# Attention pass of a graph network: who frees the PSUM buffer of the running maximum

## The reference

```python
for i in range(L):                                   # L = 4
    Q = _ln(h @ Wq[i], gq[i], bq[i])
    K = _ln(h @ Wk[i], gk[i], bk[i])
    qi, kj = Q[src], K[dst]
    score = (qi * kj).sum(-1) + 0.1 * (edge_attr * qi[:, :RBF]).sum(-1) + logm[dst]
    smax = jax.ops.segment_max(score, src, num_segments=N)
    es = jnp.exp(jnp.minimum(score - smax[src], 20.0))
    denom = jax.ops.segment_sum(es, src, num_segments=N)
    alpha = es / (denom[src] + 1e-10)
    m = h[dst] @ Wm[i]
    aggi = jax.ops.segment_sum(alpha[:, None] * m, src, num_segments=N)
    ...
```

## Time and profile before

| | us |
|---|---|
| median of 3 runs | 21067.08 |
| profiled execution, its time | 21034.33 |
| profiled execution, its span | 21032.7 |
| DVE busy | 11429.2 (54%) |
| PE busy | 11005.1 (52%) |
| POOL busy | 9367.2 (45%) |
| ACT busy | 4877.2 (23%) |

### The profile page before, as it was taken

How to read it: one execution, slowest core, us unless ns; L and a number is a source line. 1 busy time by engine, 2 the same in 40 slices (tenths; PEclk the granted TensorE clock), 3 DMA queues, 4 the chain that set the end, 5 groups by cost and what they waited for, 6 DMA issues and landing times. The chain is left out here.

```text
span 21032.7 us, 411461 instructions
## 1 busy us (share of the span) xinstructions
PE 11005.1 (52%) x122618; PEld 8580.4 (41%) x122618; DVE 11429.2 (54%) x28337; ACT 4877.2 (23%) x14465; POOL 9367.2 (45%) x10949
## 2 busy tenths in 40 slices
PE   1000056666666558847875884787155555433333
PEld 1000033333333148746865784686133333223233
DVE  4055045555555738865883886588223323256758
ACT  0000022222222034424432442443022222211110
POOL 5677755555555014413431441343344444465370
PEclk9995555555555569968986997898566666655556
DMA  8986544444445354425434442643111111134334
GB/s 60 91 178 145 61 63 63 64 66 65 64 64 66 70 157 121 122 69 174 122 91 146 125 123 65 178 123 95 54 38 37 42 38 40 34 103 131 120 114 130
DMA packets 2671465, 1951.71 MB, mean 93 GB/s; under 512 B 787834, under 2 KB 2449042, under 8 KB 2670285
## 3 DMA queue, kind: packets, MB, share of 16 engines
q1 hardware_dynamic: 1922578, 1150.35, 22.3%
q0 software_dynamic: 309216, 536.66, 14.9%
q10 hardware_dynamic: 439512, 262.80, 6.4%
HBM read 1287.52 MB, written 723.39 MB: 96 GB/s over the span
## 5 line engine op out<-in xcount | busy, mean ns | idle before, releaser
L592 POOL DMA_INDIRECT edges_rows<-raw,edges_perm_now x1824 | 1871.0, 1026 | 1582.8 <-DVEq L1163 626.0
L592 POOL DMA_INDIRECT attend_rows<-key_rows,attend_fetch_now x1824 | 1826.8, 1002 | 1047.8 <-POOL attend_fetch_now L1573 724.6
L592 POOL DMA_INDIRECT keys_rows<-table,keys_staged x1564 | 1683.5, 1076 | 548.2 <-issue 483.6
L1638 PE MATMUL attend_seg<-attend_rows,attend_hot 128*128 128x49 f32 x14592 | 1808.3, 278 | 70.1 <-issue 47.9
L1638 PEld LDWEIGHTS attend_seg<-attend_rows,attend_hot 128*128 128x128 f32 x14592 | 1720.6, 194 | 100.7 <-issue 82.0
L592 POOL DMA_INDIRECT mlp_xin<-table,mlp_staged x1564 | 1520.4, 972 | 499.4 <-issue 463.7
L1693 DVE TENSOR_REDUCE attend_mraw<-attend_top 128x2 f32<-128x1024 f32 x912 | 1114.1, 1222 | 531.0 <-remote 343.1
L2281 DVE COPY mlp_val<-mlp_ps 128x192 f32<-128x192 f32 (+1 forms) x414 | 143.3, 346 | 2295.4 <-DMA hots_lanes<-dst_lanes 1328.6
L598 POOL DMA_INDIRECT messages<-spread_out,spread_place_now x912 | 1202.0, 1318 | 394.3 <-issue 340.2
L1025 PE MATMUL edges_ps<-edges_w,edges_act 49*128 49x48 f32 x3648 | 870.9, 411 | 910.0 <-ACT edges_act L1096 872.3
L1025 PEld LDWEIGHTS edges_ps<-edges_w,edges_act 49*128 49x128 f32 x3648 | 810.6, 324 | 959.4 <-issue 958.5
(11 more groups left out here) (511 smaller groups left out, 26390.2 us busy)
## 6 DMA issues: line engine op xcount, KB each, us to landing
key_rows<-expand_out ACTq DMA_DIRECT2D x304, 624.0 KB
attend_ea<-edge_attrs SPq DMA_DIRECT2D x912, 160.0 KB
tally_rows<-messages SPq DMA_DIRECT2D x152, 864.0 KB, 4.8
expand_oht<-dst_hots SPq DMA_DIRECT2D x304, 384.0 KB, 3.5
attend_oht<-src_hots SPq DMA_DIRECT2D x912, 128.0 KB
attend_lane_hot<-src_hots_by_edge SPq DMA_DIRECT2D x912, 128.0 KB
raw<-keys_rows ACTq DMA_DIRECT2D x46, 1445.0 KB
messages<-keys_zeros SPq DMA_DIRECT2D x171, 384.0 KB
```

The source lines that it names most:

```text
L592: return nc.gpsimd.indirect_dma_start(out=out, out_offset=None, in_=table, in_offset=bass.IndirectOffsetOnAxis(ap=index, axis=0))
L1638: ins = mm(seg2[:, u, 0:SUMS], hot[p % 2][:, u, c, :], rows4[p][:, u, c, 0:SUMS], start=(c == 0), stop=(c == GR - 1))
```

## The change

A new semaphore `s_free` is raised by the maximum (L1693) itself. PE's far matmuls wait for it rather than for `s_most`. The maximum no longer counts in DVE's chain, so L1696 doesn't wait for it; L1698, which reads `mraw`, gets a wait for `s_free` of its own. The number of chained instructions in six steps falls from 8 to 7 each. `s_most`, and PE's wait for it before `back` (L1623), stay.

```diff
-        s_step, s_now, ..., s_dve_turn, s_act_turn = (ph.sem(n) for n in (
+        s_step, s_now, ..., s_dve_turn, s_act_turn, s_free = (ph.sem(n) for n in (
...
                     if live(n, 1):
                         p = (b - 1) % RING
-                        after(pe, s_most, n - 1)
+                        after(pe, s_free, n - 1)
                         pe.sem_inc(s_pe_turn, 1)
                         for u in range(2):
                             mm(top[:, u, :].rearrange("m (c q) -> m c q", c=GR), k.far[:], ..., start=True, stop=False)
...
                     if live(n, 1):
                         dve.wait_ge(s_top, n)
-                        ch.step(v.tensor_reduce(mraw[:], top[:], AX, ALU.max))
+                        v.tensor_reduce(mraw[:], top[:], AX, ALU.max).then_inc(s_free, 1)
                     ch.wait()
                     if live(n, 0):
                         ch.step(v.tensor_reduce(score[b % 3][:]...., prod[:]...., AX, ALU.add))
                     if live(n, 1):
+                        dve.wait_ge(s_free, n)
                         ch.step(v.tensor_scalar(mb[one][:, :, 0], mraw[:], -FAR_OFF, None, ALU.add))
...
-                n0, per = ch.n, 8 * RING
+                n0, per = ch.n, 7 * RING
```

More of the change, by code:

```diff
@@ L1547, in attend @@
         back, seg = ph.ps("back", [P, 512]), ph.ps("seg", [P, 512])
-        s_step, s_now, s_q, s_score, s_top, s_most, s_back, s_arg, s_exp, s_hot, s_seg, s_ev, s_table, s_pe_turn, s_pool_turn, s_share, s_hota, s_dve_turn, s_act_turn = (ph.sem(n) for n in (
-            "s_step", "s_now", "s_q", "s_score", "s_top", "s_most", "s_back", "s_arg", "s_exp", "s_hot", "s_seg", "s_ev", "s_table", "s_pe_turn", "s_pool_turn", "s_share", "s_hota", "s_dve_turn", "s_act_turn"))
+        s_step, s_now, s_q, s_score, s_top, s_most, s_back, s_arg, s_exp, s_hot, s_seg, s_ev, s_table, s_pe_turn, s_pool_turn, s_share, s_hota, s_dve_turn, s_act_turn, s_free = (ph.sem(n) for n in (
+            "s_step", "s_now", "s_q", "s_score", "s_top", "s_most", "s_back", "s_arg", "s_exp", "s_hot", "s_seg", "s_ev", "s_table", "s_pe_turn", "s_pool_turn", "s_share", "s_hota", "s_dve_turn", "s_act_turn", "s_free"))
         s_load, s_rows, s_lane = ([ph.sem(f"{n}{b}") for b in ring] for n in ("s_load", "s_rows", "s_lane"))
```

## The result

| | before, median of 6 | after, median of 6 | ratio (95% interval) |
|---|---|---|---|
| time, us | 21055.97 (21031.45 to 21076.49) | 20953.34 (20919.5 to 21006.24) | 0.9953 (0.9936 to 0.9971) |

The change gains 103 us, or 0.47%; the forecast was 55 us (0.26%). The profiled execution of after is its slowest of the six: 21006.24 us, span 21004.6. It began its first attention pass 37 us later than the execution of before did (first maximum at 7917.5, before at 7880.3), in stages that the change doesn't touch, so the spans don't show the gain. The attention passes do: over the same kind of windows as in the earlier trace rows they sum to 4702 us, against 4786.

The account below looks back on a forecast made before the run. A two-step ring of waits through POOL's second gather was taken to bound the attention passes. DVE's earlier L1696 gave 52 us, steps not held 3, the rest 0: 55 us off 21067, so 21012 us, range 20870 to 21120.

Parts of the forecast that it names:

- The ring through the second gather: Attention passes: a two-step ring of waits, maximum, ex, seg, second gather, maximum, sets the pace: 10.43 us for two steps.
- a gather is a bystander: Drawn from the skill's SBUF rule: POOL's gathers wouldn't delay the maximum, and rival 1's plain reading would hold.
- Far's move: PE's far waits for the maximum, not L1710; top starts 0.33 us earlier in step B, but price on the ring 0.
- Rival 1: Plain chain: top's start sets the maximum; 183 us gain, 20884 us, chance 0.12; whole wait gone, 20540 us, 0.03.
- rival 4: s_most (L1623) or s_score (L1614) holds PE as before; time is that of the forecast, chance 0.58 together with it.
- L1696 earlier by 0.115 us: DVE: with the maximum off the chain, L1696 and all behind it up to L1724 come 0.115 us earlier; bounds 0 to 0.12.
- Rival 2: DVE's L1696 stays or gains only 0.034 us: 0 to 16 us, 21051 to 21067 us; chance 0.13.
- The wait at L1698: DVE's new wait for s_free, covered by about 0.8 us of L1696: priced 0, from 0 to 0.18 us.
- Rival 3: The new wait holds L1698 and all behind it by 0.18 us: 82 us slower, 21149 us; chance 0.10.
- the share of steps that no gather holds: Some 5% of the attention steps gain the whole 0.115 us: 3 us more.
- the ring has DVE's part once in two steps: Attention passes: 0.115 us counts half, 0.058 us per step, times 912 steps: 52 us.
- The forecast's own sign: Profile after: idle time before the maximum grows from 527 us by about 50, as the ring gives back half of DVE's gain.

Follow-up runs that it names:

- the moved gather: Kernel after, with POOL's second gather of a step issued only behind back: 20798.04 us, ratio 0.9795; same edit in kernel before, other chip: 18795.02 us, ratio 1.0073.
- the silent POOL: Kernel after without POOL's gathers in the attention passes, SP fetching other rows: 18500.35 us, ratio 0.9914; on a signal-holding chip 20295.76 us, ratio 0.9632.
- the whole: The kernel after, unchanged, run once more beside its two halves, against the kernel before: 21093.58 us, ratio 0.9934.
- the vector engine's half: Kernel after, but far waits for s_most again; the maximum stays out of DVE's chain: 21116.99 us against 21229.0 before, ratio 0.9945.
- the control: Kernel before's order, with L1696 waiting for s_free as well as the chain and far for s_most: 18720.36 us against 18660.16 before, ratio 1.0029.
- the first group: Runs on one chip of both halves, the kernel after and its second gather moved; the kernel before took 21229 us there.
- the matrix engine's half: Kernel after, but L1696 waits for s_free too; far released early: 21352.45 us, ratio 1.0058 to before; once more on another chip 18707.25 us, ratio 1.0019.
- the third group: Kernel after and kernel after without POOL's gathers, on a chip that holds signals: 20983.74 and 20295.76 us against 21072.88 before.
- the second and the last group: Groups on chips that don't hold signals; the kernel before took 18660 us in each.

## Why the prediction was right, and where its size was off

What bounds the kernel: right, for the chips on which it was measured. The ring through the second gather was read from the order in time alone; the moved gather and the silent POOL show that the gathers are the cause of the wait. The Trainium skill's page SBUF — State Buffer, section "SBUF: two separate sides", says that PE never waits on anyone. It says so of the ports to that memory, and PE's matmuls are indeed no slower on the first chip (those of top 220 ns, on the second 219); what comes late is their signal, of which the section says nothing. What the prediction drew from it, that a gather is a bystander, fits the second chip and not the first, where the measurement decides. That a chip could do one or the other I hadn't thought of.

Far's move, priced at 0: right within what the runs can tell. Its wait went from 536.8 us to 8.2, and the idle time before the maximum didn't fall. The half alone gained nothing, and the whole is 23 us ahead of the vector engine's half, within noise. Rival 1, at 183 us, is out. Of rival 4 a part is true, at no cost in time: PE now waits for the score instead (337.1 us of L1716, in the result's rows).

L1696 earlier by 0.115 us: right. From the starts in the trace it follows the maximum by 1.140 us in the mean rather than 1.256, and its idle time is gone. Rival 2 is out: without the wait the next reduction starts 0.08 us before the first has ended, with a wait 0.03 us after. The Trainium skill's page VectorE: DVE Perf Modes, section "The DRAIN you can't avoid", measured that a semaphore between two copies costs nothing extra. The same section also says that a next instruction that isn't held starts earlier, which the prediction left out; for this pair of reductions the trace agrees with that, and not with the first.

The wait at L1698 (now L1699), priced at 0: right. The row of L1699 has no idle time before it. Rival 3 is out; the control shows what a wait costs in front of L1696, where nothing covers it: 0.068 us a step.

The term that was mis-sized is the share of steps that no gather holds, 5% and 3 us of the sum, for which no row was given, and with it "the ring has DVE's part once in two steps" as the whole of the gain. The sum gave 55 us; 103, 135 and 89 us were measured, the lower ends of their intervals at 61, 102 and 63 us. Had the ring alone counted, the idle time before the maximum would have grown by some 50 us, half of the 105 us that L1696 comes earlier in all; it grew by 15. The forecast's own sign was missed there.

I took the ring apart over all pairs of steps, from the starts in both traces. From a maximum to the start of seg it is 4.465 us before and 4.326 after: 0.139 less, about 0.12 of it on DVE, the rest on ACT. In one of two steps that is 63 us over the passes, near the forecast's 52. From seg's end to the next maximum but one it is 3.988 and 3.931, where I had taken no change: another 26 us. The two make 89 of the 97 us that the passes gained.

That second piece is a mean of two kinds: held (about 4.05 us, 92% of the cases before, 90% after) and not held (under 3.9 us, 6.4% and 9.9%). In the other traces on such chips the share of steps not held is 19.3% and 12.1% (the two later ones of after), 12.0% (the vector engine's half) and 1.9% (the matrix engine's half, in which DVE is slower). So my 5% isn't a constant. That the change raises it is argued only: there is one trace of before on such a chip, and three of the same kernel after lie between 9.9% and 19.3%. On the one chip of the first group the kernel with the slower DVE has 1.9% of them, and the two with the faster one have 12.0% and 19.3%. Why is argued, too: with a shorter step, top ends sooner after seg, and more often ahead of a second gather that is itself late.

A smaller part is in the small steps behind L1696. L1708 (now L1709), for whose end L1715 waits, took 192.0 us before and 160.3 after; without a gather beside it, it takes 171 and 172 ns, and with one 248 ns before and 179 after. The reason isn't shown.

## What to carry to other kernels

A wait that ends a fixed time after some third engine's instruction, whatever the named producer did, belongs to that third engine: set the start of the waiting instruction against the ends of all others before pricing the wait. An instruction that leaves a counted chain gives more than its place in the count, as its neighbour can start before it ends; put the wait for it on the one reader, behind something long. And where two chips differ by a tenth on the same program, run the halves of a comparison on one of them, and look at which kind it is before believing a fix: the moved gather gains 1.4% over the kernel after on one kind and loses 0.7% against the kernel before on the other. The clock of the very stage belongs in such a comparison, too: two kernels of one group had it at 0.97 and 1.00 in the same pass.

## What the runs showed of the hardware

On the chips of the result, of the first and of the third group, a signal of PE that falls due while POOL issues a gather comes only 0.6 to 0.7 us after the gather's end; on those of the second and the last group it comes at once (6.9 us of idle time against 531.0, 18660 against 21056 us). Whether it is the chip itself or how it is set up, and what makes the difference, the traces don't show.

It isn't top alone. The signal of `back`, from the matmuls behind it, is late in the same way (0.84 us in the median before, 0.70 us after a gather's end), but L1701, which waits for it, has no idle time before it. The signal of seg is on time (0.01 us), and that says nothing against the hold: POOL's gathers wait for seg, so only 5 of 912 segs end in the midst of one.

The work itself isn't slowed: seg takes its 1.96 us beside a gather, and L1696 903 ns on both chips. L1708 is an exception, with 211 ns on the first and 173 on the second. The granted clock in these passes is 0.99 to 1.00 on both for the kernel before. It is not so in every run: 0.97 to 0.98 in the matrix engine's half, with 258 us at 1.2 GHz.
